# First layer of a two-layer image network: the inverse 8x8 Fourier product as four 64x64 quarters, on a tile that ScalarE writes twice

## The reference

```
h = einsum('oi,bihw->bohw', w_in, gn(x))            # 64 -> 3*170 channels
gate, x_sp, x_fr = split(h, 3)
sp = depthwise_conv3x3(x_sp, w_dw)
xp = x_fr in patches of 8x8 pixels
fr = irfft2(rfft2(xp) * fft_weight)                 # per patch and channel
x  = x + w_out @ (gelu(gate) * (sp + fr))           # 170 -> 64 channels
```

## Time and profile before

| | |
|---|---|
| median of 3 runs | 10315.48 us (10314.36 to 10318.55) |
| profiled execution, own time | 10316.4 us |
| its span in the trace | 10314.6 us |
| mean granted TensorE clock | 0.961 of full speed |
| TensorE (PE) busy | 9562.4 us, 93% |
| TensorE weight loads (PEld) | 6862.8 us, 67% |
| VectorE (DVE) | 8275.8 us, 80% |
| ScalarE (ACT) | 5478.1 us, 53% |
| GpSimd (POOL) | 1790.3 us, 17% |

### The profile page before, as it was taken

How to read it: one execution, slowest core, us unless ns; L and a number is a source line. 1 busy time by engine, 2 the same in 40 slices (tenths; PEclk the granted TensorE clock), 3 DMA queues, 4 the chain that set the end, 5 groups by cost and what they waited for, 6 DMA issues and landing times.

```text
span 10314.6 us, 161555 instructions
## 1 busy us (share of the span) xinstructions
PE 9562.4 (93%) x60966; PEld 6862.8 (67%) x60966; DVE 8275.8 (80%) x12487; ACT 5478.1 (53%) x8535; POOL 1790.3 (17%) x1824
## 2 busy tenths in 40 slices
PE   1899998999899998998989999899898999989998
PEld 1777765656677776565667777565566777756555
DVE  7788878878688887887868888787886888878786
ACT  0455544555655554454765555445475555445556
POOL 0000003333300001333320000233341000032333
PEclk6999999999999999999999999999999999989999
DMA  4666666575676776557566677646666666574655
GB/s 113 145 138 142 141 134 206 173 227 157 159 146 138 143 142 165 179 172 235 155 153 142 138 145 142 197 157 197 187 179 129 126 126 130 114 226 160 213 167 155
DMA packets 1332434, 1650.03 MB, mean 160 GB/s; under 512 B 844604, under 2 KB 1076684, under 8 KB 1246284
## 3 DMA queue, kind: packets, MB, share of 16 engines
q1 hardware_dynamic: 1331660, 1639.70, 63.4%
HBM read 786.45 MB, written 514.86 MB: 126 GB/s over the span
## 4 chain that ended last, share of the span: by engine, by line
PE 81%; DVE 10%; issue 3%; ACT 3%; DMA 1%; POOL 1%; SPq 1%; DVEq 0%; ACTq 0%; POOLq 0%
PE ps L821 15%; PE ps L1747 14%; PE ps L1760 7%; PE ps L791 6%; PE ps L1771 5%; PE ps L851 4%; PE ps L782 4%; PE ps L835 4%; DVE S L1527 3%; PE ps L875 2%; PE ps L862 2%; PE ps L1395 2%; PE ps L797 2%; PE ps L1316 2%; PE ps L815 2%
## 5 line engine op out<-in xcount | busy, mean ns | idle before, releaser
L1133 DVE SCALAR_TENSOR_TENSOR F<-U,LW,F 106x512 f32<-106x512 f32 x2048 | 1536.0, 750 | 54.4
L1747 PE MATMUL ps<-fp,Dwr 128*128 128x512 f32 x6144 | 1546.6, 401 | 0.0
L1747 PEld LDWEIGHTS ps<-fp,Dwr 128*128 128x128 f32 x6144 | 1115.5, 188 | 613.5 <-ACT x L1836 292.1
L1111 DVE TENSOR_TENSOR Z<-ps,LW 128x340 f32<-128x340 f32 x1024 | 523.1, 511 | 820.4 <-PE ps L791 819.5
L945 ACT ACTIVATE XF<-ps 128x340 f32<-128x340 f32 x1024 | 464.5, 454 | 1116.6 <-PE ps L782 1116.6
L821 PE MATMUL ps<-P,WP 128*128 128x512 f32 x3072 | 904.6, 416 | 31.0 <-DMA H<-P 31.0
L821 PE MATMUL ps<-H,WP 128*128 128x512 f32 x3072 | 918.3, 421 | 0.0
L1395 PE MATMUL ps<-fp,Bwr 128*128 128x512 f32 x3072 | 877.1, 425 | 21.3 <-DVE fp L1496 21.3
L1836 ACT ACTIVATE x<-ps,cst 128x512 f32<-128x512 f32 x512 | 351.8, 687 | 1014.2 <-PE ps L1760 1010.3
L1760 PE MATMUL ps<-XP,Cwr 128*128 128x512 f32 x3072 | 803.9, 398 | 76.7 <-DVE XP L1882 76.7
L1051 POOL TENSOR_SCALAR xo<-xo 64x512 f32<-64x512 f32 x4 | 6.0, 1500 | 4900.1 <-DVE xo L1167 4900.1
(11 more groups left out here) (299 smaller groups left out, 19851.4 us busy)
## 6 DMA issues: line engine op xcount, KB each, us to landing
H<-P SPq DMA_DIRECT2D x512, 585.0 KB, 7.2
raw<-x SPq DMA_DIRECT2D x240, 640.0 KB, 11.5
fx_d<-fx SPq DMA_DIRECT2D x112, 1024.0 KB, 3.9
fl_d<-fp SPq DMA_DIRECT2D x112, 1024.0 KB, 5.6
fp<-fl_d SPq DMA_DIRECT2D x112, 1024.0 KB, 6.5
fx<-fx_d SPq DMA_DIRECT2D x112, 1024.0 KB, 5.6
x1h_d<-xo SPq DMA_DIRECT2D x256, 256.0 KB, 9.0
x1v_d<-xo SPq DMA_DIRECT2D x512, 128.0 KB, 7.8
```

Source lines behind the costliest of these rows:

```text
L1111: e.tensor_tensor(Z[t % 2][:, 2 * c:2 * c + 2, :].rearrange("p a b -> p (a b)"), ps[6][:, 0:2 * HID], Wt, ALU.mult).then_inc(sem["z"], 1)
L1133: ins = e.scalar_tensor_tensor(o, u, wd[0:106, i:i + 1], o, ALU.mult, ALU.add)
L1747: ins = e.matmul(bank(m)[:], Dwr[:, w, c:c + 128], fq[n % 2][x][:, s2, :], start=(s2 == 0 and w == 0 and x == 0), stop=False)
```

## The change

- `Rinv`, the 128x128 inverse matrix, goes. `Rblk` (128x64: the 64x64 inverse matrix R twice, one below the other) and `R42` (128x128, for the 42 channels) take its place; one more DMA loads them for each image.
- A group of 128 pixels in `xb` is now an 8x8 patch of the left 64 columns and the one 64 columns to its right. So `blocks` needs four copies of 64x512 and not two of 64x1024.
- `finv` is one step for both halves: for each of the 8 groups, for each half i (64 partitions of Z, bank `ps[2 + i]`) and each half of the channels, one product of a 64x64 stationary with 64 moving columns. That is 32 products where there were 8 of 128x128 with 128 columns. It stands where xs(t+1,1) stood; the two old places are empty.
- The gate and the last convolution tap need rows in plain order, which `xb` no longer gives for one half; ScalarE writes the tile a second time, `xr` (`rows`, two copies of 64x1024, two buffers, a new semaphore `xr`).
- VectorE's `fu(t, 0)` moves from ahead of z(t+1, 0) to just ahead of `fu(t, 1)`.
- `finv42` keeps its 16 products of 64 columns, with another order of columns.

The second layer is not touched.

```diff
-    Rinv, Rfwd = at("Rinv", [128, 128]), at("Rfwd", [128, 128])
+    Rblk, R42, Rfwd = at("Rblk", [128, 64]), at("R42", [128, 128]), at("Rfwd", [128, 128])
...
+    xr = [at(f"xr{i}", [128, 8, 128], F32R) for i in range(2)]
...
         def gate(t, i):
             e.wait_ge(sem["uc"], 3 * (NT * b + t) + i + 1)
-            m = xb[t % 2][:, 512 * i:512 * i + 512].rearrange("p (k r w) -> p r k w", k=4, r=8)
+            e.wait_ge(sem["xr"], NT * b + t + 1)
+            m = xr[t % 2][:, :, 64 * i:64 * i + 64]
...
-        def finv(t, i):
-            o = ps[2 + i][:].rearrange("p (r c) -> p r c", r=8)
-            for j in range(4):
-                if j % 2 == 0:
-                    e.wait_ge(sem["z"], 4 * (NT * b + t) + 2 * i + j // 2 + 1)
-                ins = e.matmul(o[:, :, 16 * j:16 * j + 16], Z[t % 2][:, 4 * i + j, 0:128], Rinv[:], start=False, stop=(j == 3))
-            ins.then_inc(sem["fi"], 1)
+        def finv(t):
+            for k in range(8):
+                if k % 2 == 0:
+                    e.wait_ge(sem["z"], 4 * (NT * b + t) + k // 2 + 1)
+                for i in range(2):
+                    hf = slice(64 * i, 64 * i + 64)
+                    o = ps[2 + i][:].rearrange("p (r k c) -> p r k c", r=8, k=8)[:, :, k, :]
+                    for q in (slice(0, 64), slice(64, 128)):
+                        ins = e.matmul(o[q], Z[t % 2][hf, k, q], Rblk[hf, :], start=False, stop=(k == 7))
+                    if k == 7:
+                        ins.then_inc(sem["fi"], 1)
...
-            finv(t, 0)
             xs(t + 1, 0)
             if t:
                 conv(t, 1, range(3))
             fs(t + 1, 0)
             if t:
                 conv(t, 1, range(3, 5))
+            finv(t)
             xs(t + 1, 1)
-            finv(t, 1)
             if t:
                 gate42(t)
...
             for p in range(2):
                 hf = slice(64 * p, 64 * p + 64)
-                dst = xb[t % 2][hf, :].rearrange("c (k r w) -> c r k w", k=8, r=8)
-                src = P[t % 2][p][hf, 1:9, 1 - p:129 - p].rearrange("c r (k w) -> c r k w", w=16).bitcast(F32)
-                ins = e.activation(dst, src, ACT.Copy)
+                for i in range(2):
+                    c = 64 * i + 1 - p
+                    dst = xb[t % 2][hf, :].rearrange("c (k i r w) -> c i r k w", k=8, i=2, r=8)[:, i]
+                    src = P[t % 2][p][hf, 1:9, c:c + 64].rearrange("c r (k w) -> c r k w", w=8).bitcast(F32)
+                    ins = e.activation(dst, src, ACT.Copy)
             ins.then_inc(sem["xb"], 1)
+
+        def rows(t):
+            if t >= NT:
+                return
+            for p in range(2):
+                hf = slice(64 * p, 64 * p + 64)
+                src = P[t % 2][p][hf, 1:9, 1 - p:129 - p].bitcast(F32)
+                ins = e.activation(xr[t % 2][hf], src, ACT.Copy)
+            ins.then_inc(sem["xr"], 1)
...
         blocks(0)
+        rows(0)
         p1(e, b, 1)
...
         blocks(1)
+        rows(1)
         for c in range(1, 4):
...
             blocks(t + 2)
+            rows(t + 2)
...
         for t in range(NT):
-            fu(t, 0)
             z(t + 1, 0)
             depthwise(t, range(4, 7))
+            fu(t, 0)
             fu(t, 1)
```

More of the change, by code:

```diff
@@ L82, in constants @@
     R = np.array(basis)
[L83 to L88, removed]
+    Rb = np.kron(np.eye(2), R)
+    k["k_R42"] = Rb.reshape(128, 2, 4, 2, 8).transpose(0, 3, 2, 1, 4).reshape(128, 128)
+    k["k_Rblk"] = np.concatenate([R, R], 0)
     k["k_Rfwd"] = Rb.T
@@ L720, in ahead_0 @@
         e.dma_start(Rfwd[:], a["k_Rfwd"]).then_inc(sem["rt"], 16)
-        e.dma_start(Rinv[:], a["k_Rinv"]).then_inc(sem["rt"], 16)
+        e.dma_start(Rblk[:], a["k_Rblk"]).then_inc(sem["rt"], 16)
+        e.dma_start(R42[:], a["k_R42"]).then_inc(sem["rt"], 16)
     def l0_sp(e, b):
@@ L812, in conv @@
                 if j == 4:
-                    m = xb[t % 2][:, 512 * i:512 * i + 512].rearrange("p (k r w) -> p r k w", k=4, r=8)
+                    if i == 0:
+                        e.wait_ge(sem["xr"], NT * b + t + 1)
+                    m = xr[t % 2][:, :, 64 * i:64 * i + 64]
                     for p in range(2):
@@ L857, in finv42 @@
                 e.wait_ge(sem["ad"], NT * b + t)
-            R = Rinv[:].rearrange("k (a p c) -> k p a c", a=4, p=2)
+            R = R42[:].rearrange("k (p a i w) -> k p a i w", p=2, a=4, i=2)
             for k in range(8):
                 for p in range(2):
-                    o = ps[4][64 * p:64 * p + HL, :].rearrange("p (a c) -> p a c", a=4)
-                    ins = e.matmul(o[:, :, 16 * k:16 * k + 16], Z[t % 2][:, k, 128:HID], R[:, p], start=True,
+                    o = ps[4][64 * p:64 * p + HL, :].rearrange("p (a i k w) -> p k a i w", a=4, i=2, k=8)
+                    ins = e.matmul(o[:, k], Z[t % 2][:, k, 128:HID], R[:, p], start=True,
                                    stop=True, skip_group_check=True)
@@ L881, in l0_pe @@
         e.wait_ge(sem["wp"], b + 1)
-        e.wait_ge(sem["rt"], 32 * (b + 1))
+        e.wait_ge(sem["rt"], 48 * (b + 1))
         if b:
```

## The result

The changed kernel took **10253.57 us** (median of 4 runs, 10250.26 to 10255.01); the kernel before, run beside it, 10315.43 us. The ratio is 0.9938, with a 95% interval of 0.9926 to 0.9950: 62 us faster, where 109 were forecast (10207, range 10160 to 10290). The profiled execution took 10252.34 us.

A forecast was written before the change was run, and what follows sets the result against it. TensorE's stream of products was taken as the bound. Per tile 0.58 - 0.10 - 0.03 = 0.45 us, by 256 tiles 115 us, less 6 at image starts, 109: from 10316.4 to 10207 us, range 10160 to 10290.

The forecast's parts named there:

- The bound: First layer, steady tiles: TensorE's stream of products sets the time, 18.79 us from gate to gate; VectorE and ScalarE are less busy.
- What goes, 1.80 us: TensorE, per tile: the two old finv steps, 0.80 and 0.84 us, plus 0.09 and 0.07 by which they lengthened xs and gate42.
- finv, 1.22 us: TensorE, per tile: the new finv costs 1.22 us including entering and leaving, priced from finv42's row; saving 0.58 us.
- the step on which the sign rested: New finv on TensorE: all four 64x64 quarters run at once, giving 1.22 us; only in pairs it would be 2.25.
- fs(t+1, 1), 0.10: TensorE, per tile: with finv gone from behind xs(t+1, 1), this fs waits for ScalarE's copy, costing 0.10 us (0 to 0.2).
- ScalarE, 0.03: Added copies ahead of G and XF(t+1, 0) use up ScalarE's idle time; charged 0.03 us per tile, between 0 and 0.30.
- ScalarE comes late: Rival: XF(t+1, 0) ends 0.30 us after TensorE wants it in each tile; 10276 us, chance 0.12.
- VectorE, free: VectorE has the same work, 15.9 us per tile against a period of 18.3; moving fu(t, 0) costs nothing.
- Start of an image, 6 us: At each image's start rows(1) stands ahead of XF(0, 1), making it 1.4 us late, four times, 6 us.
- Sum: Whole kernel: 0.45 us saved per tile by 256 tiles, 115 us, less 6 is 109, giving 10207 us.
- The low end of the stated range: Whole kernel: 10165 us, the case with no wait at all, 0.58 x 256 = 148 us saved.
- The rule on records: New finv: at 25 ns per record, 64 records need 1.60 us, 1.79 with edges, about 32 us slower in all; not adopted.

## Why the prediction was right, and by what it was off

**The bound.** Right: TensorE busy 999.96 of 1000 us before and 999.92 after, VectorE and ScalarE below. At the starts of the images TensorE also waits for `xb` (31 us in four waits), which the prediction did not list; it is 32 us after the change.

**What goes, 1.80 us.** Nothing contradicts it: the booking above closes to 0.01 us with it.

**finv, 1.22 us.** Measured 0.08 + 1.09 + 0.11 + 0.01 = 1.29. That all four quarters run at once was the step on which the sign rested; 1.09 against 1.84 us in pairs shows it. Mis-sized by 0.07: finv42's row carries 42 weight columns, the quarters 64, and the step looked at moving columns alone (0.04 of it, shown by the run with 42); the other 0.03 lies in the edges and was not taken apart.

**fs(t+1, 1), 0.10.** Measured 0.09, and the run that covers it gives back 0.11.

**ScalarE, 0.03.** Measured 0.11, the largest error. From the start of the copies to the end of XF the sum had 5.87 us, and the trace has 5.94: the four small copies hold ScalarE 2.36 us to the start of rows and not 2.19, as they overlap less than those of `columns`, rows 2.15 and not 2.13, while XF starts 0.12 ahead of the end of the gates G, which the sum did not use. XF was to end 0.14 us ahead of fs (1034.42 and 1034.56) and ends 0.06 ahead, and this 0.08 is what the wait costs more than forecast, in full. The rival "ScalarE comes late" was the right mechanism at a third of its price of 0.30. That ScalarE's queue makes the wait is shown by moving rows; the share of the small copies is an estimate.

**VectorE, free.** Right as it stands; with fu in its old place it would have cost some 420 us, a price that the prediction had not given.

**Start of an image, 6 us.** About 1.5 to 2 us for each image in this trace: right.

**Sum.** 0.58 - 0.10 - 0.03 became 0.51 - 0.09 - 0.11 = 0.31; by 256 that is 79 us, less 6 is 73, and the first layer's share in the two traces is 72. The measured 62 us is less by what the rest of the program took more in these executions; the cause of that was not tested. 109 us forecast against 62 measured, 47 short: 18 by finv, 20 by ScalarE, about 10 outside the first layer, less a little that the other terms gave back. The low end of the stated range has a slip: 10316 less 148 is 10168, and with the 6 us of the starts 10174, not 10165.

**The rule on records.** The sentence that start-to-start never drops below about 25 ns (the Trainium skill, TensorE: Matmul & The Clock Gate, "Wait — 56ns, not 53.3ns?") does not hold across quarters: 64 records in 1.09 us are 0.017 us each, 64 in 0.68 are 0.011. For records of one and the same tile of the array no run here shows it.

## What to carry to other kernels

A product whose matrix is block-diagonal wastes the array. Cut into quarters, with both row halves and both column halves in flight, the two steps of 1.64 us became one of 1.09, if the issue order rotates through the four; through two it took 1.84. Each stay among small tiles costs 0.3 to 0.4 us to enter and leave here, the neighbours' part included. When a long step shrinks or moves, list every waiting step that it used to cover and every consumer that now comes too early. Here two waits of 0.1 us took 40% of the gain of a steady tile, two reorderings of issue gave them back, and one line left in its old place would have turned 0.6% faster into 3.5% slower.

## What was not expected of the hardware

Copies of 64x512 on ScalarE took 2.33 us for four in blocks and 2.19 in `columns`, with the same sizes; the difference is the one step where blocks goes over to the other 64 partitions (0.64 us from start to start, against 0.52 to 0.54). Two copies of 64x1024 on different 64 partitions did not overlap at all (1.07 us from start to start, 1.06 long). That the partitions are the cause was not tested apart. Switching straight from 64x64 quarters to 128x64 halves left both steps as long as before (1.10 + 1.02 against 1.09 + 1.03 us); only the neighbours gained, 0.13 us. GpSimd's 110 copies per 1000 us left VectorE's records as they were (0.750 us for a tap in both).
